# A two-layer cross-attention network on one core: overlapped stage borders, and the projections of Q and K ahead of the value products

## What is computed

```python
x = x + _L0_xattn_ref(_layernorm(x), ctx_1024, ctx_1024, ...)
x = x + _L0_ffn_ref(_layernorm(x), ...)
x = x + _L1_xattn_ref(_layernorm(x), ctx_1024, ctx_1024, ...)
x = x + _L1_ffn_ref(_layernorm(x), ...)
```

## Time and profile before

| | us |
|---|---|
| three runs | 1018.84, 1021.54, 1021.41 |
| median | 1021.41 |
| the profiled execution, its own time | 1020.8 |
| its span in the profile | 1018.7 |
| PE busy | 942.4 (93%) |
| ACT busy | 774.9 (76%) |
| DVE busy | 699.0 (69%) |
| POOL busy | 378.0 (37%) |

### The profile page before, as it was taken

One profiled execution on the slowest core, in us unless ns is written; L12 is line 12 of the kernel. 1 busy time (PEld: TensorE's weight loads), 2 busy tenths in 40 slices (PEclk: granted clock), 3 DMA queues, 4 the chain that ended last, 5 costly groups with the idle time before them and its releaser, 6 DMA issues. The chain is left out here.

```text
span 1018.7 us, 32982 instructions
## 1 busy us (share of the span) xinstructions
PE 942.4 (93%) x12352; PEld 727.5 (71%) x12352; DVE 699.0 (69%) x1916; ACT 774.9 (76%) x1473; POOL 378.0 (37%) x571
## 2 busy tenths in 40 slices
PE   5899999999949999999999999889999999979998
PEld 3577777877637877888878887556676767658886
DVE  7578888887755666666677665366565665568995
ACT  3387788888837888888888888457777777658996
POOL 7679999999520100000000000344444444011110
PEclk9799999999979999999999999999999999989999
DMA  6321322211000000000000000122222221100111
GB/s 256 116 64 59 116 61 63 61 48 38 18 1 1 1 0 0 0 0 0 0 0 0 0 1 1 37 67 65 59 65 60 64 62 57 30 2 22 41 41 62
DMA packets 43812, 41.73 MB, mean 41 GB/s; under 512 B 24096, under 2 KB 32288, under 8 KB 43296
## 3 DMA queue, kind: packets, MB, share of 16 engines
q1 hardware_dynamic: 42384, 31.75, 10.0%
q10 hardware_dynamic: 1296, 8.14, 2.1%
HBM read 16.79 MB, written 4.19 MB: 21 GB/s over the span
## 5 line engine op out<-in xcount | busy, mean ns | idle before, releaser
L790 DVE TENSOR_REDUCE top<-ps_w 128x16 f32<-128x1024 f32 x128 | 156.4, 1222 | 122.9 <-PE ps_w L495 122.8
L971 PE MATMUL g_ps<-g_h_lo,w_hi 128*128 128x512 f32 x512 | 204.9, 400 | 0.0
L972 PE MATMUL g_ps<-g_h_hi,w_hi 128*128 128x512 f32 x512 | 203.3, 397 | 0.0
L1185 DVE TENSOR_TENSOR g_h_lo<-g_h,g_h_hi 128x512 fp32r<-128x512 f32 x192 | 132.6, 691 | 92.0 <-ACT g_h_hi L1134 88.1
L132 POOL TENSOR_TENSOR front_rstd<-front_spread,minus_half 128x4 f32<-128x4 f32 x32 | 33.4, 1043 | 402.8 <-DVE front_spread L125 402.8
L622 ACT ACTIVATE prob_t<-ps_w 128x1024 f32<-128x1024 f32 x128 | 131.2, 1025 | 45.4 <-PE ps_w L498 45.4
L495 PE MATMUL ps_w<-qk_sets,qk_t 32*64 32x256 f32 x2048 | 145.0, 393 | 5.2 <-DMA qk_sets<-qk_t 5.2
L1134 ACT ACTIVATE g_h_hi<-g_h 128x512 fp32r<-128x512 f32 x192 | 121.4, 632 | 18.5 <-DVE g_h L1195 14.4
L498 PE MATMUL ps_w<-qk_sets,qk_t 32*64 32x256 f32 x2048 | 133.9, 375 | 1.0 <-issue 1.0
L736 POOL TENSOR_SCALAR normed<-x_res,moments,rstd 128x128 f32<-128x128 f32 x116 | 96.5, 837 | 69.9 <-PE ps_turn L513 69.7
L972 PEld LDWEIGHTS g_ps<-g_h_hi,w_hi 128*128 128x128 f32 x512 | 96.6, 189 | 22.8
(11 more groups left out here) (157 smaller groups left out, 2083.7 us busy)
## 6 DMA issues: line engine op xcount, KB each, us to landing
qk_sets<-qk_t SPq DMA_DIRECT2D x256, 64.0 KB, 1.9
ctx_in<-in_ctx SPq DMA_DIRECT2D x32, 128.0 KB, 2.6
ctx_in<-in_ctx_t SPq DMA_DIRECT2D x32, 128.0 KB, 2.7
out_x<-x_res SPq DMA_DIRECT2D x16, 256.0 KB, 2.0
x_res<-in_ff_weights ACTq DMA_DIRECT2D x1, 2560.0 KB, 16.1
shift<-pieces SPq DMA_DIRECT2D x128, 16.0 KB, 2.4
x_res<-in_x ACTq DMA_DIRECT2D x1, 1792.0 KB, 7.0
x_res<-in_x ACTq DMA_DIRECT2D x1, 1536.0 KB, 7.7
```

Of the source, the lines that this page charges most:

```text
L790: nc.vector.tensor_reduce(out=top[:, i % 2, half, :], in_=bank_pair(half).rearrange("p (a q) -> p a q", q=SEQ), op=ALU.max, axis=AX.X).the ...
L971: nc.tensor.matmul(out, w_hi, x_lo, start=first and w_lo is None, stop=False)
L972: return nc.tensor.matmul(out, w_hi, x_hi, start=False, stop=last)
L1185: nc.vector.tensor_tensor(h_lo[level][:, o, :], h[:, o % 2, :], h_hi[level][:, o, :].bitcast(F32), ALU.subtract).then_inc(lo_ready[level], 1)
```

## The change

There are five parts.

1. **Q and K first.** In PE's step of both attentions the projections of Q and K (unit j+2) move from behind the heads' transposes to before the value products, and in ACT's step their copy moves from behind the copies of the value products and heads to directly behind the first exponential.
2. **The first units of the second attention are prepared in the gated feed-forward.** The Front there goes on for one more chunk (index N, data of chunk 0, which is final by then): statistics, power, normalised rows and PE's transposes, into `t.ps_turn`, PSUM that the stages now share. These are units 0 and 1 of the second attention (`READY = 2`), where their own steps are left out; ACT copies them from there.
3. **The first products of the last stage move into the second attention.** `first_products` runs the twelve matmuls of chunk 0 in two halves after steps N+3 and N+4, into the shared `t.ps_w`; `plain_feed_forward` begins with chunk 1.
4. **The register holds the opposite.** DVE turns the largest low part of each partition into 1.0 where it is zero; the smallest of these is read, and the program without low parts now stands first in the code, straight behind the branch.
5. **Fillers.** The table `FILL` changes in both layers.

```diff
-FILL = ({(-3, 0): 5, (-1, 1): 6, (1, 0): 2, (1, 1): 6},
-        {(-3, 0): 12, (-2, 0): 2, (-1, 1): 8, (0, 0): 2, (1, 0): 2, (1, 1): 6})
+FILL = ({(-3, 0): 4, (-2, 0): 2, (-1, 0): 2, (-1, 1): 13, (0, 1): 8, (1, 0): 2, (1, 1): 6},
+        {(-3, 0): 4, (-2, 0): 2, (-1, 0): 2, (-1, 1): 8, (0, 0): 2, (1, 0): 2, (1, 1): 6})
...
+    READY = 0 if gated else 2
...
-                    if on(i):
-                        pe.wait_ge(normed_ready, i + 1)
+                    if on(i) and i >= READY:
+                        pe.wait_ge(normed_ready, i + 1 - READY)
...
+                def first_products(outputs):
+                    pe.wait_ge(front.x_lo_ready, 1)
+                    pe.wait_ge(exp_done, 2 * N)
+                    for o in outputs:
+                        cols = slice(o * P, (o + 1) * P)
+                        last = split_products(nc, ps_w[:, o * 512:(o + 1) * 512], t.w_hi[:, FF0_GROUPS, cols], t.w_lo[:, FF0_GROUPS, cols],
+                                              front.x_hi[:, 0, :], front.x_lo[:, 0, :], True, True)
+                        last.then_inc(front.up_done, 1)
...
                     lead(j, 0)
+                    i = j + 2
+                    if on(i):
...
+                        pe.wait_ge(turned_taken, i + 1)
+                        wait(pe, qk_taken, i)
+                        wait(pe, v_taken, upto(j + 1))
...
+                        nc.tensor.matmul(ps_mid[:, 0:UNIT], wq, turned[:, i % TURNED, 0, :], start=True, stop=True)
+                        nc.tensor.matmul(ps_mid[:, UNIT:2 * UNIT], wk, from_ctx, start=True, stop=True).then_inc(qk_done, 1)
                     i = j - 3
...
                     step(j)
+                    if not gated and j >= N + 3:
+                        first_products((0, 1) if j == N + 3 else (2, 3))
...
-                        nc.tensor.transpose(ps_mid[0:1, 0:P], t.lo_max[:, :], t.ident[:, :]).then_inc(lo_row_ready, 1)
+                        nc.tensor.transpose(ps_mid[0:1, 0:P], t.lo_none[:, :], t.ident[:, :]).then_inc(lo_row_ready, 1)
...
-                    t.lo_bits = pe.value_load(t.lo_bits_row[0:1, 0:1].bitcast(I32))
+                    t.lows_absent = pe.value_load(t.lo_bits_row[0:1, 0:1].bitcast(I32))
...
-                        act.wait_ge(in_t_done, i + 1)
+                        if i >= READY:
+                            act.wait_ge(in_t_done, i + 1 - READY)
+                        at = 0 if i >= READY else i * UNIT
...
+                        dve.wait_ge(lo_largest, 1)
+                        nc.vector.tensor_scalar(t.lo_none[:, :], t.lo_max[:, :], 0.0, None, ALU.is_equal).then_inc(lo_largest, 1)
...
-                        if ahead(j + 1):
+                        if ahead(j + 1) or following(j + 1):
                             front_turn_in(nc, t, front, pe, j + 1, 0, ps_in)
...
-                with pe.If(t.lo_bits):
+                with pe.If(t.lows_absent):
+                    program(with_lo=False)
+                with pe.Else():
                     program(with_lo=True)
-                with pe.Else():
-                    program(with_lo=False)
...
+                    if following(j + 2):
+                        front_measure(nc, t, front, dve, N, 0, chunk=0)
...
+                    if following(j + 2):
+                        front_normalise(nc, t, front, dve, N, 0, chunk=0)
...
-                    if on(j):
+                    if ahead(j):
                         wait(pe, front.x_lo_ready, j + 1)
```

104 lines of the change are left out of this document (52 added, 52 removed).

## The result

The changed kernel takes **1024.3 us** (median of 20 runs, 1019.2 to 1028.2) beside 1018.6 for the kernel before in the same measurement (20 runs, 1009.7 to 1023.6): a ratio of **1.0062, interval 1.0042 to 1.0081**. I had forecast 1015.0 with a range up to 1021.5. Single runs of either kernel lie up to 9 us from their median, more than any part of the change was forecast to be worth; so times are told with the interval of their ratio to the kernel before, and the parts are read from the profiles.

What follows compares the result with a forecast made beforehand. The prediction took PE's own work and order to bound the kernel. Its terms, +2 - 4.5 + 0 - 2.5 - 3.0 - 0.5 + 2.2 = -6.3 us, gave a median of 1015.0, range 1008.0 to 1021.5.

Steps and rivals of the forecast that it cites:

- What bounds the kernel: Both attentions: PE is fullest, 50.00 and 46.86 of 50 us, so its order and holes decide.
- Part 1: Both attentions, Q and K projected before the value products: +2 us in the first, 0 in the second.
- the ring: Second attention: each step's loop through PE, ACT and DVE, where every PE piece counts; claimed to keep its length, 0.
- Part 2: PE's stops at fixed places, every 256 instructions: first attention -4.5 us (-6.0 + 1.5), second attention 0.
- Part 3: Start of the kernel: changed fillers hold PE at its upper clock level; -2.5 us, ends -3.6 and +1.
- Part 4: Border into the gated feed-forward: PE starts some 0.15 us behind DVE, its program following the branch; together -3.0 us.
- Part 5: Border into the second attention: projections earlier -2.5, transposes +0.4, lower clock level +1.6; together -0.5 us.
- the first rival: Border into the second attention: the branch stall moves to the short program's end; +2.7 us, 1017.7, chance 0.12.
- Part 6: Border into the last stage: it waits for the first chunk's twelve products, whose early making saves nothing; +2.2 us.
- The slower rival: First attention: `turned` late by more, at 0.5 us a step 13 us instead of 2, 1026.0; chance 0.11.
- named for right: Signs in steps, holes, start and borders that would confirm the forecast, such as steps of 7.2 to 7.3 and 6.93 us.
- named for wrong: Signs against: first-attention step over 7.5 us, equal holes in the second score piece, PE missing 3 us at second border.

Runs made afterwards that it cites:

- e15: The kernel before with two more small operations on POOL in every unit of the first attention: 1025.7 us, ratio 1.0121.
- e1: The changed kernel with the projections of Q and K put back behind the value products, on PE and ACT: 1022.4 us, ratio 1.0048.
- e2: The kernel before with only the projections of Q and K moved ahead of the value products, on PE and ACT: 1014.1 us, ratio 1.0008.
- e3: The changed kernel with the order value products, projections of Q and K, heads' transposes: 1018.4 us, ratio 1.0028.
- e7: The changed kernel with the order projections of Q and K, heads' transposes, value products: 1018.3 us, ratio 1.0023.
- e12: The kernel before with 36 instructions that do nothing added at the head of PE's program, shifting the code behind: 1019.6 us, ratio 1.0026.
- e5: The changed kernel with the last stage's first chunk of products put back behind its border: 1020.2 us, ratio 1.0035.
- e6: The changed kernel with `lo_none` put into the same 32 bytes as `lo_max`, so that it shifts no later tile: 1026.0 us, ratio 1.0094.

## Why the prediction was wrong, point by point

**What bounds the kernel.** PE "is busy 50.00 of 50 us", "with every other engine further from full": true, and misread. POOL's 47.44 in the same row was a second bound, and its distance from full was no distance from binding (e15: +10.2 us of stage). The first stage ended at 283.58 instead of 283.43, though PE's steps got longer and its holes fewer.

**Part 1, the order in the ring: the step that failed.** "Nothing is added to PE: the same matmuls in another order, 2.26 us from the end of A to B in either", and "so the ring keeps its length: 0". The 2.26 for the new order was never read from a row. From A's last piece to B it was 2.58 before and 2.83 after. Not the matmuls but what lies between them changed. In the second stage it is 0.20 a step (7.13 beside 6.93), which e1 and e2 switch off and on, e3 and e7 cut to 0.05: 5.8 us in 29 steps, put at nothing. The stage became 4.3 longer in the two profiles; other kernels with this order and other holes have 217.0 to 219.5, so part of the 4.3 belongs to the holes. In the first, 0.06 of the 0.25 is `turned` (0.08 forecast); there 2 us were forecast and some 6 came in steps. They did not lengthen the stage, which POOL ended.

**Part 2, the holes.** Right in kind: places in the code. In the first stage the 6.0 went, as forecast, and one of 1.7 us came, in the output product, where the count had none, with 1.8 us of a lower clock behind it. Of +2 - 4.5 for both parts the stage shows -1.6: the steps took the holes' gain, and e12, which has it alone, got only 2.3 of 6.0 because of POOL. The Trainium skill, "Runtime: NRT & Kernel Launch", section "Instruction fetch mechanics", calls such crossings mostly hidden; the holes of 0.7 to 1.7 us in e12 and in both kernels disagree.

**Part 3, the start.** -2.5 forecast; the first value product came 1.7 later, and over 18 profiles its mean is 51.9 with the old fillers and 53.1 with the new: no gain shows. What varies is the granted clock: from 20 to 52 it was 0.73 in the profile before, 0.79 after, and 1.00 in e2, with the old fillers (the kernel before, then e2; busy us of PE, PEld, DVE, ACT, POOL, then the clock):

```profile
20.00:52.00 32.00, 25.90 (x223) 16.59 (x223) 19.00 (x60) 14.74 (x40) 23.14 (x32) 0.73 0.31 104
```
```profile
20.00:52.00 32.00, 29.48 (x423) 19.66 (x423) 23.41 (x74) 20.92 (x55) 28.71 (x42) 1.00 0.37 125
```

I had taken one execution's start for the kernel's.

**Part 4, the border into the gated feed-forward.** Right: -3.0 forecast, -3.1 measured from the last output product.

**Part 5, the border into the second attention.** -0.5 forecast, +1.8 measured (from the last transposes to the first value product 36.0 us instead of 34.2). This is the first rival, given a chance of 0.12 and 2.7 us: the stall of the branch at the other end is 2.5, and the early units give 0.7 back. The terms of the part itself were near: the first projection stands at 652.65 instead of 655.78, 2.7 closer to the fillers (-2.5 forecast), and from it to the first value product are 2.0 more (+1.6 forecast). The step that failed here is the stall, left out of the sum because PE could "run ahead".

**Part 6, the border into the last stage.** +2.2 forecast, +2.33 measured, undone by e5. The last stage behind it, up to its last transposes, is 0.6 longer (the spacing alone gives 1.3), and the last store 1.1, neither forecast.

**The rivals.** The slower rival named the right term, the step, with a wrong cause (`turned`) and for the wrong stage. The sum by the profiles, where the start and the noise of one execution each are in it:

| stretch | forecast | profiles |
|---|---|---|
| start | -2.5 | +1.7 |
| first attention | -2.5 (+2 - 4.5) | -1.6 |
| border into the gated feed-forward | -3.0 | -3.1 |
| gated feed-forward | 0 | 0 |
| border into the second attention | -0.5 | +1.8 |
| second attention | 0 | +4.3 |
| border into the last stage | +2.2 | +2.3 |
| last stage and last store | 0 | +1.7 |
| sum | -6.3 | +7.2, the difference of the spans (rows rounded) |

The largest misses are the second attention (4.3), the start (4.2, which one profile of each kernel can't tell from the spread of starts) and the border into the second attention (2.3).

**The signs.** Of those named for right, no hole in the value products of the first stage is left (true), the 16 matmuls of the scores take 1.09 at 32.84 (true, though 1.98 again at 37.17), the first product of the gated feed-forward comes 0.18 behind DVE's first (289.65, 289.47; true), the first projection 3.1 earlier (true) and DVE 3.83 instead of 1.50 behind the last attention product (true). The steps of 7.40 and 7.13 for 7.2 to 7.3 and 6.93 are false. Of those named for wrong, "PE missing at the second border for 3 us" came: 3.50.

## What to carry to other kernels

When pieces are put in another order on TensorE, count the changes between full-size products and small tiles, not only the matmuls: keep the full-size ones in one block. Before costing a stage by its fullest engine, ask of each engine that is nearly full in it (POOL had 95% here) how long a unit takes it; two bounds close to each other can swallow a change that moves only one. When a branch past a long program stalls, swapping the two programs moves the stall to the other end: cost both ends. And more than one profile of the same kernel is needed before a start or a low stretch of the clock is called the kernel's.

## What had not been expected of the hardware

- A hole in TensorE's instruction stream ends 1.2 to 1.6 us after the fetch of 16 KB that it goes with (eleven holes of the kernel before), and 36 instructions at the head of a program move it.
- Shifting the operands of 512-column products by 32 bytes changed their spacing between 229.6 and 233.2 ns in the last stage, both ways (after, e6); the gated feed-forward kept 233.2 to 233.3 with either. Why was not tried.
- From the last transposes to the end are 4.7 to 5.2 us in the ten profiles with the changed borders, and 3.9 to 4.2 in the other eight. In the ten, an instruction fetch of another queue starts 1.3 to 1.7 us ahead of the last packet of the last store; in the eight it starts behind it. This is argued from its time; no run separates it. The DMA pages of the last store, before and after (KB, us from issue to landing; and the fetch: packets, MB):

```profile
out_x<-x_res SPq DMA_DIRECT2D x1, 256.0 KB, 2.0
```
```profile
q14 instruction: 1, 0.01, 1.2%
out_x<-x_res SPq DMA_DIRECT2D x1, 256.0 KB, 3.1
```
